# Unread TensorE products in seven waits of each batch row, and 80 instead of 58 of them behind the last row

## What is computed

```python
proj = hidden @ W_in.T                       # gate, x, B, C, dt
hBC  = silu(causal_conv4(proj_xBC) + b)      # 4 taps along the sequence
h    = exp(dt*A) * h + (dt*x) B              # 32 heads, state 64 x 128, over 512 steps
y    = (h C + D*x) * silu(gate);  y = rmsnorm(y) @ W_out.T
f    = (sigmoid(n @ Q(w1).T) * (n @ Q(w2).T)) @ Q(w3).T     # Q: ternary weights
a    = softmax(q k / 4 + alibi + causal) v @ W_o            # 16 heads of 16
idx, w = router(n)                           # 64 experts, best 6 of the best 4 groups
m    = sum_k w_k * expert_k(n) + shared(n)   # relu^2 experts, at most 64 slots each
```

## Time and profile before

| | |
|---|---|
| median of three runs | 1371.82 us |
| profiled execution | 1371.9 us, of which the span from first to last instruction is 1370.1 us |
| mean granted TensorE clock | 0.937 |
| PE busy | 1145.9 us (84%) |
| DVE, ACT, POOL busy | 912.0, 658.6, 567.1 us |
| FFN of rows 0 to 3 begins (first L1300) | 210.21, 508.18, 805.47, 1100.27 us |
| expert stage on PE | 1257.91 to 1315 us |

### The profile page before, as it was taken

How to read it: one execution, slowest core, us unless ns; L and a number is a source line. 1 busy time by engine, 2 the same in 40 slices (tenths; PEclk the granted TensorE clock), 3 DMA queues, 4 the chain that set the end, 5 groups by cost and what they waited for, 6 DMA issues and landing times.

```text
span 1370.1 us, 24377 instructions
## 1 busy us (share of the span) xinstructions
PE 1145.9 (84%) x8378; PEld 741.5 (54%) x8380; DVE 912.0 (67%) x1850; ACT 658.6 (48%) x1575; POOL 567.1 (41%) x725
## 2 busy tenths in 40 slices
PE   2799998898899888988999988989999978877940
PEld 2355556665555557655555566655555566644520
DVE  4487785565788875656888875656887755671427
ACT  3655423666455524656445335666555235630630
POOL 1255561220377760210577831200777712133760
PEclk9999999999999998998999998999999999989975
DMA  7366442300243314101343332001333625058888
GB/s 312 118 206 196 156 156 74 94 2 20 87 145 108 107 43 118 48 2 35 120 129 101 116 80 70 25 21 39 129 123 106 195 76 162 10 196 268 155 198 313
DMA packets 120137, 159.56 MB, mean 116 GB/s; under 512 B 11632, under 2 KB 82928, under 8 KB 119280
## 3 DMA queue, kind: packets, MB, share of 16 engines
q1 hardware_dynamic: 106384, 131.73, 31.0%
q0 software_dynamic: 9216, 19.98, 5.7%
q10 hardware_dynamic: 4416, 6.29, 1.3%
HBM read 104.55 MB, written 40.83 MB: 106 GB/s over the span
## 4 chain that ended last, share of the span: by engine, by line
PE 55%; DVE 19%; POOL 7%; issue 7%; ACT 6%; DMA 4%; SPq 0%; POOLq 0%; DVEq 0%; ACTq 0%
PE bank L1187 12%; PE bank L1229 5%; DVE pool_c L1689 5%; PE bank L1110 5%; PE bank L1410 3%; PE bank L1367 3%; PE bank L1395 2%; PE bank L1332 2%; PE bank L1223 2%; PE bank L1216 2%; PE bank L1208 2%; PE bank L1300 2%; POOL joint L2198 2%; PE bank L1497 2%; POOL xn L2205 2%
## 5 line engine op out<-in xcount | busy, mean ns | idle before, releaser
L1187 PE MATMUL bank<-xm,joint 128*128 128x512 f32 x544 | 272.8, 626 | 20.2 <-DVE pool_c L1689 15.6
L2198 POOL TENSOR_TENSOR joint<-joint 128x512 f32<-128x512 f32 x128 | 168.5, 1318 | 225.3 <-DVE joint L1705 221.2
L1689 DVE SCALAR_TENSOR_TENSOR pool_c<-bank,params,pool_c 128x511 f32<-128x511 f32 (+2 forms) x216 | 161.1, 747 | 84.8 <-ACT pool_c L812 79.4
L1187 PEld LDWEIGHTS bank<-xm,joint 128*128 128x128 f32 x544 | 99.9, 197 | 123.9 <-issue 93.3
L1889 DVE TENSOR_REDUCE nmax<-bank 128x1 f32<-128x384 f32 (+3 forms) x176 | 109.6, 637 | 60.6 <-PE bank L1368 59.8
L1229 PE MATMUL bank<-wout,pool_c 128*128 128x256 f32 x512 | 125.1, 388 | 3.4 <-DVE pool_c L1730 3.4
L851 ACT ACTIVATE joint<-bank,dt_ 128x64 f32<-128x64 f32 x512 | 112.0, 342 | 28.7 <-PE bank L1110 28.7
L1229 PEld LDWEIGHTS bank<-wout,pool_c 128*128 128x128 f32 x512 | 98.6, 196 | 38.7 <-issue 23.3
L821 ACT ACTIVATE pool_c<-pool_c 128x512 f32<-128x512 f32 x64 | 40.2, 629 | 143.5 <-DVE pool_c L1689 143.5
L2192 POOL DMA_INDIRECT xslot<-xrow,slots x96 | 97.3, 1013 | 26.6 <-issue 21.9
L1730 DVE TENSOR_TENSOR pool_c<-xn,pool_c 128x512 f32<-128x512 f32 x64 | 90.0, 1405 | 19.1 <-POOL xn L2205 19.0
(11 more groups left out here) (272 smaller groups left out, 2379.1 us busy)
## 6 DMA issues: line engine op xcount, KB each, us to landing
pool_b<-dA_rows SPq DMA_DIRECT2D x64, 256.0 KB
pool_b<-dec_rows SPq DMA_DIRECT2D x96, 128.0 KB, 3.6
joint<-pool_b SPq DMA_DIRECT2D x96, 128.0 KB, 2.4
acc<-xrow SPq DMA_DIRECT2D x13, 640.0 KB, 6.1
joint<-dA_rows SPq DMA_DIRECT2D x32, 256.0 KB, 3.2
dA_late<-dA_rows SPq DMA_DIRECT2D x32, 256.0 KB, 4.1
joint<-acc SPq DMA_DIRECT2D x32, 256.0 KB, 6.7
xslot<-xrow SPq DMA_DIRECT2D x16, 321.0 KB, 4.8
```

The costliest lines, as they stand in the source:

```text
L1187: last = mm(bank[:, :], win[:, k, col:col + P], xm[:, k, :], start=(k == 0), stop=(k == KD - 1))
L1689: ins = v.scalar_tensor_tensor(out=cv[:, n:L], in0=bank[:, 0:L - n], scalar=convw[:, ci, TAPS - 1 - n:TAPS - n], in1=cv[:, n:L], op0=ALU.m ...
L2198: M_ready.inc(p.tensor_tensor(M[u % 2][:, hs_, :], Lx[:, hs_, :], cbm[:, c * P:(c + 1) * P].unsqueeze(1).to_broadcast([P, 4, P]), ALU.mult))
```

## The change

Seven calls of `stay_awake` are put into PE's list and the count of the existing one is raised from 58 to 80. In this text the places have numbers: 1 (4 products) and 2 (4) in the FFN, 3 (9) ahead of `norm_T(2, 0)`, 4 (3) and 5 (3) around `norm_T(2, 1)`, 6 (8) ahead of `norm_T(3, 1)`, 7 (8) ahead of the shared expert's down products, 8 at the end of the last row. Rows 0 to 2 pass all of 1 to 7 (39 products each); the last row has no `between` and passes 1 to 5 (23 products). With the 22 more at the end that is 162 products.

```diff
@@ ffn @@
                 mean_squares(1)
+                stay_awake(4, pb[5])
                 pe.wait_ge(ln_done.sem, ln_done.upto(pair_count(b, 1, 0)))
                 at(h_lo_done, 1)
                 for n in range(2 * FT + 2):
                     p_, f = divmod(n, FT)
+                    if n == 2:
+                        stay_awake(4, pb[5])
                     if n == 4:
                         norm_T(1, 1)
...
                     if n == FT + 3:
+                        stay_awake(9, pb[5])
                         norm_T(2, 0)
@@ second_queries @@
+                stay_awake(3, pb[2])
                 norm_T(2, 1)
+                stay_awake(3, pb[2])
                 queries_keys(1, 0)
@@ finish @@
-                stay_awake(58, pb[3])
+                stay_awake(80, pb[3])
@@ between @@
                 m(project_in, ("x", 0, 0))
+                r(stay_awake, 8, pb[5])
                 r(norm_T, 3, 1)
...
                 m(turn_in, ("T", 0, 1))
+                r(stay_awake, 8, pb[2])
                 r(shared_down, 0)
```

## The result

The changed kernel takes 1349.96 us (median of 6 runs, 1346.77 to 1357.13) against 1372.12 us of the kernel before on the same chip (6 runs, 1371.51 to 1373.66): ratio 0.9844, 95% interval 0.9821 to 0.9866, 22 us off. Two things have to be kept in mind. The runs of the kernel before agree within 2.2 us, those of the changed kernel are spread over 10. And the profiled execution is the slowest of the six (span 1354.4, mean granted clock 0.959, against 0.937 before), so its trace shows some 7 us less gain than the median. One of all executions, 2243.2 us in the run without places 6 and 7, lies far outside its kernel's others and enters no ratio.

The account below looks back on a forecast made before the run. PE, 55% of the chain, was taken to lose time at clock 0.50 behind its waits. Terms 2.5 + 6.9 + 3.2 + 4.6 + 3.4 + 0.5 = 21.1 us off 1371.9 gave 1350.8, range 1341 to 1362.

Parts of the forecast that it names:

- Places 1 and 2: FFN start: clock falls go in row 0 (1.5 us) and row 3 (1.0), nothing in rows 1 and 2; 2.5 us.
- Place 3: Ahead of `norm_T(2, 0)`: up and down products regain full clock, 1.73 us in each of four rows; 6.9 us.
- Places 4 and 5: Around `norm_T(2, 1)`: two rows without a fall gain 3.8 us, one with it loses 0.6, row 3 nothing; 3.2 us.
- Place 6: Router stretch behind `norm_T(3, 1)`: of 8.2 us clock loss, two falls of 1.8 remain in three rows; 4.6 us gained.
- place 7: Shared expert's down products: no fall left, rows 0 and 2 gain 1.69 us each; 3.4 us.
- Place 8: End of last row, before the expert stage: clock falls a little later; 0.5 us gained, ends 0 and 1.8.
- Falls elsewhere: Next mixers' starts and last attention: falls not touched but shift against the work, some 2 us either way.
- transposes don't count: Rival: transposes leave places 4 to 6 empty for the clock, all falls there stay; 11.5 us off, 1360; chance 0.22.
- slower: Rival: products run at half speed in the waits and outlast them; 18 us lost, 1390; chance 0.04.
- nothing: Rival: the falls stay and the products hide in the waits; 1372; chance 0.04.
- Every fall goes: Rival: no clock fall remains at any of the places; 30.0 us off, 1342; chance 0.15.
- The next engine is the bound: Rival: DVE absorbs half of the gain, above all behind place 7; 10.5 us off, 1361; chance 0.12.

## Why the prediction was right, and where its sum was not

The direction, the way and the total held: 21.1 us forecast, 22 found, 1350.8 against 1349.96. The products hold the clock from inside the waits and are hidden by them (row 0's 1.75, 0.79, 0.58 and 0.45 us are left over); doubled, they cost; halved, they give about half. The parts of the sum did not hold, and the total came out to 1 us by errors that cancel, which is luck:

- **Places 1 and 2** (2.5): the stretch gave 2.8 as worked out row by row; taken out they cost 8.4, with falls at the router beside those in their own stretch. The term saw only its own stretch.
- **Place 3** (6.9, "the firmest term"): this is the step that failed, twice. In its stretch three rows gave 1.2 us each, not four 1.73: up and down products gain as counted, but PE then waits for ACT's `xnT`, so the queries start only 1.24 us sooner (235.36 - 231.72 = 3.64 for 236.38 - 231.50 = 4.88 in the before trace), and row 3, whose wait was 3.56 us before and not row 0's 2.74, fell all the same in the two traces of the changed kernel. "All of it is PE work in line" overlooked that wait. And in the whole it is worth nothing alone, where other falls in the row lengthen by as much, and less than some 3 us beside the others (1350.42 without it).
- **Places 4 and 5** (3.2): no row of 0 to 2 kept its fall; 5.7 in the trace, 6.4 by the run without them. The guess of one fall in three was too careful, the floor of 3.4 us right.
- **Place 6** (4.6) and **place 7** (3.4): 5.9 and 3.4 in the trace, 10.4 together by the run without them. One router fall remained in three, not two; in other traces none did.
- **Place 8** (0.5): nothing in the first trace, where 80 leave 4.02 us; 98 leave none, and even these give 1 us, less than can be told.
- **Falls elsewhere** ("some 2 us either way"): the new fall in the mixer costs 0.95 us in row 0 and 0.70 in row 1.

Of the rivals, *transposes don't count* is refuted by the run with transposes, *slower* and *nothing* by the result. *Every fall goes* (1342) did not come true, even with more products at most places: 1347.3 to 1348.2. *The next engine is the bound* has a share: ACT's 0.27 us at place 3, DVE's 0.60 us ahead of the second queries, DVE's running sum in the last row. Of the signs named beforehand row 0's FFN stretch (15.3: 15.25), the up groups (1.04), the down products in all rows (3.72) and the router (20.7: 20.88) came; 1.00 behind `norm_T(2, 0)` came in three rows of four.

What stays open: why the same code has a fall in one execution and none in another, why place 3's gain is taken up by the other falls to 0.06 us a row, why an early fall is followed by one 110 us later, and so why the runs' values (8.4 + 0.4 + 6.4 + 10.4 = 25.6 us, above the 22 of all together) are not those of the single stretches.

## What to carry to other kernels

Filler products in a wait are free as long as they end before the wait does, and in most places here they keep the clock for what follows; count them by the wait (0.22 us each here) and leave no long rest behind them. But judge each place by a run without it, not by its own stretch: a fall that goes can lengthen or make the next one, so a single place may be worth nothing and another two or three times what its stretch shows. And take more than one trace: the same code has other falls in another execution. Fill only waits ahead of work that the chain goes through.

## What the runs showed that was not expected

- f32 transposes hold the clock as unread bf16 products do (1351.29 for 1350.08 us).
- A fall some 20 us into a mixer costs nothing: behind row 1 of the kernel before, four in-projections take 2.87 us behind a wait of 2.24 us for DVE, with 98 at the end they take 1.98 behind the same wait, and the time from the down products' end to the next FFN is 149.65 and 149.63 us. Of the ten mixers behind rows 0 and 1 that have no later fall, in all fourteen traces, six with this one take 149.64 to 149.67 us and four without it 149.63 to 149.69. With a fall some 104 us into them the other eighteen take 150.35 to 151.94.

```profile
674.85 2.87 PE L1187 MATMUL bank<-xm,joint 128*128 128x512 f32 x4 [2.24 <-DVE pool_c L1689]
```

```profile
662.13 1.98 PE L1187 MATMUL bank<-xm,joint 128*128 128x512 f32 x4 [2.24 <-DVE pool_c L1697]
```

- A higher mean clock is not a shorter time: 0.943 and 1371.5 us of span with place 3 alone, 0.937 and 1370.1 before; 0.965 and 1357.5 with twice the products, 0.959 and 1354.4 with the single dose.
- The changed kernel is less steady: its ten runs lie within 10.4 us, all 48 of the kernel before within 7.0. That fewer falls are the reason is not shown: the four runs with twice the products, whose trace has fewer still, lie within 1.2.
